# First stage of a four-block kernel: the gate network is multiplied into the mean weights, VectorE normalises three chunks, the orders are rewritten

## The reference

```python
x = x + _layernorm(_L0_attn_ref(_layernorm(x)))          # dilated attention, segments of 64
x = x + _layernorm(_L0_ffn_ref(_layernorm(x), weight))   # Hadamard, 4-bit activations, ternary weights
x = x + _layernorm(_L1_attn_ref(_layernorm(x), ...))     # 16 heads; rows gated, only 32 a batch
x = x + _layernorm(_L1_ffn_ref(_layernorm(x), ...))      # causal attention, 8 experts, top 2

# inside _L1_attn_ref:
q_mean = q.mean(axis=1)                                  # mean over the 16 heads: 64 numbers a token
mu, var = q_mean.mean(-1), q_mean.var(-1)
H = (q_mean - mu) * rsqrt(var + LN_EPS) * ln_g + ln_b
h = gelu(H @ w1.T + b1)                                  # 64 -> 16
scores = (h @ w2.T + b2)[..., 0]                         # one score a token, then the top 32
```

## Time and profile before

| | us |
|---|---|
| median of 3 runs | 642.27 |
| lowest, highest | 640.2, 647.02 |
| the profiled execution | 641.33 |
| its span, first to last instruction | 639.6 |

### The profile page before, as it was taken

One profiled execution on the slowest core, in us unless ns is written; L12 is line 12 of the kernel. 1 busy time (PEld: TensorE's weight loads), 2 busy tenths in 40 slices (PEclk: granted clock), 3 DMA queues, 4 the chain that ended last, 5 costly groups with the idle time before them and its releaser, 6 DMA issues. The chain is left out here.

```text
span 639.6 us, 11630 instructions
## 1 busy us (share of the span) xinstructions
PE 536.4 (84%) x3754; PEld 299.9 (47%) x3754; DVE 485.3 (76%) x2125; ACT 369.1 (58%) x829; POOL 248.8 (39%) x474
## 2 busy tenths in 40 slices
PE   1876577977989997679999999999998898999971
PEld 0876567975676563112333333333333455456420
DVE  6499878367665667889799999999997156369786
ACT  4962255610534564014687788878788665466864
POOL 2001044744001333102445454544555454266764
PEclk9987665557997998555899999999999989899996
DMA  8000000110000694200111111111110000000001
GB/s 325 9 1 2 0 34 35 66 26 8 1 2 9 169 250 130 62 3 5 32 39 37 34 38 35 55 45 39 32 40 2 7 2 1 1 2 17 17 34 66
DMA packets 18875, 27.32 MB, mean 43 GB/s; under 512 B 3230, under 2 KB 14126, under 8 KB 18638
## 3 DMA queue, kind: packets, MB, share of 16 engines
q1 hardware_dynamic: 18174, 24.34, 12.9%
q10 hardware_dynamic: 576, 2.10, 0.9%
q0 software_dynamic: 64, 0.13, 0.1%
HBM read 14.11 MB, written 12.45 MB: 42 GB/s over the span
## 5 line engine op out<-in xcount | busy, mean ns | idle before, releaser
L982 DVE CUSTOM_DVE_ANT_0 w_qkvT<-d_pS,w_qkvT 128x512 bf16<-128x512 f32 x480 | 203.9, 486 | 16.8 <-PE d_pS L973 11.7
L1651 ACT ACTIVATE d_P<-pT 128x768 f32<-128x768 f32 (+1 forms) x192 | 165.9, 882 | 62.7 <-PE pT L1677 61.0
L1531 POOL TENSOR_SCALAR_AFFINE_SELECT d_P<-d_P 128x256 f32<-128x256 f32 x256 | 103.1, 417 | 133.6 <-ACT d_P L1651 133.6
L973 PE MATMUL d_pS<-Ks,Qs 48*128 48x512 bf16 x480 | 97.9, 325 | 12.8 <-DVE hadamard L982 8.9
L1677 PE MATMUL d_pO<-d_P,V 128*32 128x512 f32 (+3 forms) x1024 | 98.5, 460 | 1.4 <-POOL d_P L1531 0.9
L1677 PE MATMUL pT<-Qs,Ks 51*128 51x512 bf16 (+3 forms) x512 | 72.8, 312 | 2.0 <-ACT d_mT L1621 2.0
L973 PEld LDWEIGHTS d_pS<-Ks,Qs 48*128 48x128 bf16 x480 | 32.3, 96 | 56.1 <-DVE hadamard L982 51.9
L1677 PEld LDWEIGHTS pT<-Qs,Ks 51*128 51x128 bf16 x512 | 20.7, 94 | 74.1 <-ACT d_P L1651 42.7
L982 DVE DVE_READ_ACCUMULATOR2_ANT hadamard<- 128x1 f32 x512 | 42.7, 83 | 0.0
L1994 ACT ACTIVATE e_T<-pT,comb 128x128 f32<-128x128 f32 x88 | 25.1, 381 | 22.7 <-issue 15.0
L1677 PEld LDWEIGHTS d_pO<-d_P,V 128*32 128x32 f32 x1024 | 21.2, 110 | 32.3 <-issue 29.5
(11 more groups left out here) (336 smaller groups left out, 1051.7 us busy)
## 6 DMA issues: line engine op xcount, KB each, us to landing
Qs<-q_stack SPq DMA_DIRECT2D x32, 192.0 KB, 3.2
q_stack<-Qp SPq DMA_DIRECT2D x8, 384.0 KB, 2.7
X<-in_x_dram ACTq DMA_DIRECT2D x4, 512.0 KB, 6.2
n_rows<-N SPq DMA_DIRECT2D x4, 512.0 KB, 2.8
q_stack<-Qp SPq DMA_DIRECT2D x8, 256.0 KB, 3.0
out_dram<-e_moe SPq DMA_DIRECT2D x8, 256.0 KB, 2.0
w_qkvT<-in_w_qkvT_dram SPq DMA_DIRECT2D x1, 1536.0 KB
Ks<-k_stack SPq DMA_DIRECT2D x32, 48.0 KB, 3.3
```

The costliest lines, as they stand in the source:

```text
L973: last = nc.tensor.matmul(dst[:, at:at + w], top.Qs[c][rows, h % 8, 128 * q:128 * q + 128], top.Ks[c][rows, h // 4 % 2, 0:w], start=True, ...
L982: last = nc.vector.tensor_tensor_reduce(out=junk[:, at:at + w], in0=src[:, at:at + w], in1=top.wide_mask[:, 512 - w:512], scale=1.0, scala ...
L1531: last = nc.gpsimd.affine_select(out=view, in_=view, compare_op=ALU.is_ge, fill=0.0, base=0, pattern=[[0, 2], [1, 128]], channel_multiplie ...
L1651: nc.scalar.activation(P[pair % 4][:, :, P_AT[unit]:P_AT[unit] + w], pT[(3 * pair + unit) % 2][:, :, 0:w], ACT.Exp, scale=float(HD4) ** -0 ...
```

## The change

The gate network is folded into the mean weights. Its gain and first layer come to a 64 x 16 matrix: the w1 columns times `ln_g`, with the centring over the 64 features applied by `spread`. With the mean weights, turned, on the other side, one product gives `fold`: 64 columns of centred mean queries and 16 columns of first-layer outputs without scale. `means` makes all 80 columns. Since the 64 columns are centred, ACT's `squares3` gives their variance; DVE scales the 16 columns by the reciprocal root and adds a constant row `offset`, made from `ln_b`, w1 and b1. `qstats`, `qnorm`, ACT's `normalise3`, `turned_z`, `gained`, PE's `gate` and POOL's `ones_row` go.

Three of the chunk normalisations are done by DVE, with one tensor_scalar a tile: the first block's of chunks 1 and 3 (from ACT), the third block's of chunk 3 (from POOL). The orders of DVE, ACT and PE are written anew. No transfer is added or taken away; SP's fourth store waits for DVE instead of POOL.

```diff
-        HT = [flat(expS[c])[0:DH + 1, :] for c in chunks]
+        pre = [nT[c][:, 3, :].rearrange("p (t k) -> p t k", k=PROJ) for c in chunks]
...
-        z = [flat(top.O4[:, CT // 2 * c:CT // 2 * c + CT // 2, :]).rearrange("p (t d) -> p t d", d=DH) for c in chunks]
...
+        turned_mean = PS[0][0:DH, 5, :]
+        gain_psum = PS[0][0:DH, 6, 0:PROJ]
+        offset_psum = PS[0][:, 7, 0:PROJ]
+        fold_psum = PS[0][:, 4, 0:DH + PROJ]
+        w_meanT = ph.sb("w_meanT", [DH, D])
+        gains = ph.sb("gains", [DH, PROJ])
+        spread = ph.sb("spread", [DH, DH + PROJ])
+        biases = ph.sb("biases", [DH + 1, D])
+        fold = ph.sb("fold", [128, DH + PROJ])
+        offset = ph.sb("offset", [128, PROJ])
...
-                    sp.wait_ge(sm["s3_n"], done[c])
+                    if c == CHUNKS - 1:
+                        sp.wait_ge(sm["s3_n_vector"], 1)
+                    else:
+                        sp.wait_ge(sm["s3_n"], done[c])
...
+                    nc.vector.tensor_scalar(spread[:, 0:DH], top.ident[0:DH, 0:DH], 1.0 / DH, None, ALU.subtract)
+                    nc.vector.tensor_scalar(gains[:, :], top.w1T[0:DH, :], top.ln_gb[:, 0:1], None, ALU.mult)
+                    dve.wait_ge(sm["ones"], 1 + 1)
+                    nc.vector.tensor_scalar(biases[0:DH, :], biases[0:DH, :], top.ln_gb[:, 1:2], None, ALU.mult)\
+                        .then_inc(sm["fold_rows"], 1)
...
                     dve.wait_ge(sm["parts_psum"], 1)
-                    dve.wait_ge(sm["centred_psum"], 1)
+                    dve.wait_ge(sm["gain_psum"], 1)
+                    nc.vector.tensor_copy(w_meanT[:, :], turned_mean)
+                    nc.vector.tensor_copy(spread[:, DH:DH + PROJ], gain_psum).then_inc(sm["turned"], 1)
+                    nc.vector.tensor_copy(offset[:, :], offset_psum).then_inc(sm["offset_row"], 1)
...
-                    nc.vector.tensor_copy(top.w_qmeanT[:, :], centred).then_inc(sm["centred"], 1)
+
+                def fold_home():
+                    dve.wait_ge(sm["fold_psum"], 1)
+                    nc.vector.tensor_copy(fold[:, :], fold_psum).then_inc(sm["fold"], 1)
...
+                def normalise1(c):
+                    for t in range(CT):
+                        last = nc.vector.tensor_scalar(n[c][:, t, :], X[c][:, t, :], mv["s1_"][c][:, t, 0:1],
+                                                       rs1[c][:, t:t + 1], ALU.subtract, ALU.mult)
+                    last.then_inc(sm["s1_n_vector"], 1)
...
-                def qstats(c):
-                    dve.wait_ge(sm["s3_qm"], done[c])
-                    moments(lambda t: PS[c][:, t, 0:DH], c, "s3_q")
-                    dve.wait_ge(sm["s3_qmv"], done[c])
+                def normalise3(c):
+                    dve.wait_ge(sm["s3_rstd"], done[c])
+                    dve.wait_ge(sm["s1_O"], done[c])
+                    for t in range(CT):
+                        last = nc.vector.tensor_scalar(n[c][:, t, :], X[c][:, t, :], mv["s3_"][c][:, t, 0:1],
+                                                       rs3[c][:, t:t + 1], ALU.subtract, ALU.mult)
+                    last.then_inc(sm["s3_n_vector"], 1)
...
+                def qvariance(c):
+
+                    dve.wait_ge(sm["s3_qss"], done[c])
                     dve.wait_ge(sm["s3_small"], done[c])
-                    nc.vector.tensor_tensor(qvar[c][:, :], mv["s3_q"][c][:, :, 1], small3[c][:, :], ALU.add)\
+                    nc.vector.scalar_tensor_tensor(out=qvar[c][:, :], in0=ss[c][:, :], scalar=1.0 / DH,
+                                                   in1=small3[c][:, :], op0=ALU.mult, op1=ALU.add)\
                         .then_inc(sm["s3_qvar"], 1)
 
-                def qnorm(c):
+                def gate(c):
+
                     dve.wait_ge(sm["s3_qstd"], done[c])
                     nc.vector.reciprocal(qrs[c][:, :], qstd[c][:, :]).then_inc(sm["s3_qrstd"], 1)
                     dve.wait_ge(sm["s3_qrstd"], done[c])
-                    nc.vector.scalar_tensor_tensor(out=qnb[c][:, :], in0=mv["s3_q"][c][:, :, 0], scalar=-1.0,
-                                                   in1=qrs[c][:, :], op0=ALU.mult, op1=ALU.mult)\
-                        .then_inc(sm["s3_qnorm"], 1)
+                    nc.vector.tensor_tensor(pre[c], PS[c][:, :, DH:DH + PROJ],
+                                            qrs[c][:, :].rearrange("p (t o) -> p t o", o=1).broadcast_to([128, CT, PROJ]),
+                                            ALU.mult).then_inc(sm["s3_gate"], 1)
+                    dve.wait_ge(sm["s3_gate"], done[c])
+                    dve.wait_ge(sm["offset_row"], 1)
+                    nc.vector.tensor_tensor(pre[c], pre[c],
+                                            offset[:, :].rearrange("p (o k) -> p o k", o=1).broadcast_to([128, CT, PROJ]),
+                                            ALU.add).then_inc(sm["s3_pre"], 1)
...
-                stats1(0); stats1(1); norm1(0); stats1(2); norm1(1); stats1(3)
-                norm1(2); ternary_weights(); norm1(3); mean_weights(); sums(0); sums(1)
+                stats1(0); stats1(1); norm1(0); stats1(2); norm1(1); normalise1(1); norm1(2)
+                stats1(3); ternary_weights(); norm1(3); normalise1(3); mean_weights(); sums(0); sums(1)
                 ostats1(0); ostats1(1); add1(0); add1(1); stats2(0); stats2(1)
                 sums(2); sums(3); variance1(2); quantise(0); variance1(3); add1(2)
-                weights_home(); add1(3); clamp(0); quantise(1); stats2(2); variance2(0)
-                quantise(2); add2(0); stats2(3); stats3(0); quantise(3); qstats(0)
-                clamp(1); qnorm(0); clamp(2); clamp(3); norm3(0); variance2(1); add2(1)
-                variance2(2); stats3(1); add2(2); norm3(1); variance2(3); stats3(2)
-                add2(3); qstats(1); qnorm(1); stats3(3); norm3(2)
-                qstats(2); norm3(3); qnorm(2); qstats(3); qnorm(3)
+                weights_home(); add1(3); fold_home(); clamp(0); quantise(1); stats2(2); clamp(1)
+                variance2(0); stats2(3); add2(0); quantise(2); variance2(1); add2(1)
+                quantise(3); clamp(2); stats3(0); clamp(3); stats3(1); norm3(0); norm3(1)
+                variance2(2); add2(2); variance2(3); add2(3); qvariance(0); stats3(2); stats3(3)
+                gate(0); qvariance(1); norm3(2); norm3(3); gate(1); normalise3(3)
+                qvariance(2); gate(2); qvariance(3); gate(3)
...
-                def normalise3(c):
-                    act.wait_ge(sm["s3_qnorm"], done[c])
+                def squares3(c):
+                    act.wait_ge(sm["s3_qm"], done[c])
                     for t in range(CT):
-                        last = nc.scalar.activation(z[c][:, t, :], PS[c][:, t, 0:DH], ACT.Identity,
-                                                    bias=qnb[c][:, t:t + 1], scale=qrs[c][:, t:t + 1])
-                    last.then_inc(sm["s3_z"], 1)
...
-                def gained(c):
...
-                    act.wait_ge(sm["s3_zT_psum"], done[c])
-                    nc.scalar.activation(HT[c][0:DH, :], PS[c][0:DH, :, :].rearrange("p t d -> p (t d)"),
-                                         ACT.Identity, bias=top.ln_gb[:, 1:2], scale=top.ln_gb[:, 0:1])\
-                        .then_inc(sm["s3_H"], 1)
+                        last = nc.scalar.activation(nT[c][:, t, 0:DH], PS[c][:, t, 0:DH], ACT.Square,
+                                                    accum_out=ss[c][:, t:t + 1])
+                    last.then_inc(sm["s3_qss"], 1)
...
                     act.wait_ge(sm["s3_pre"], done[c])
-                    nc.scalar.activation(u[c], PS[c][:, 0, :].rearrange("p (t k) -> p t k", k=PROJ), ACT.Gelu)\
+                    nc.scalar.activation(u[c], pre[c], ACT.Gelu)\
                         .then_inc(sm["s3_gelu"], 1)
...
-                std_1(0); std_1(1); normalise1(0); std_1(2); normalise1(1); normalise1(2)
-                copy1(0); std_1(3); copy1(1); normalise1(3); copy1(2); exponential(0)
-                exponential(1); copy1(3); ostd_1(0); ostd_1(1); exponential(2); exponential(3)
+                std_1(0); std_1(1); normalise1(0); std_1(2); copy1(0); normalise1(2); std_1(3); copy1(1)
+                exponential(0); exponential(1); copy1(2); copy1(3); ostd_1(0); ostd_1(1)
+                exponential(2); exponential(3)
                 copy2(0); squares1(2); std_2(0); std_2(1); squares1(3); copy2(1)
                 ostd_1(2); ostd_1(3)
-                copy2(2); copy2(3); std_2(2); squares2(0); ostd_2(0); copy3(0); std_2(3)
-                std_3(0); qstd_3(0); normalise3(0); squares2(1); ostd_2(1); squares2(2); gained(0)
-                ostd_2(2); copy3(1); std_3(1); squares2(3); ostd_2(3); copy3(2); qstd_3(1)
-                normalise3(1); std_3(2); copy3(3); std_3(3); gained(1); qstd_3(2)
-                normalise3(2); qstd_3(3); normalise3(3); gained(2); gelu(0); gelu(1); gained(3)
-                gelu(2); gelu(3)
```

(58 more changed lines are left out.)

12 lines of the change are left out of this document (5 added, 7 removed), and 6 rows, old and new, of the table sm.

## The result

The median of four runs is 620.22 us (619.95 to 624.36); the kernel before has 642.26 us. The ratio is 0.9664, 95% interval 0.9619 to 0.9708. The profiled execution took 620.27 us, 21.06 less than the one before. The predicted time, 626 us, is 5.8 us too high; it is inside its range of 619.5 to 634, near the lower end, and next to rival A (621 us).

The account below looks back on a forecast made before the run. DVE's order while busy, then a slackless chain at the end, bound the first stage. Start 5.33 + work 95.8 + gaps 3.4 + waits 10.0 gave 114.5 us, 16.1 less: 626 us, range 619.5 to 634.

Parts of the forecast that it names:

- rival A: Last normalisation of the first stage: POOL does not hold DVE's tensor_scalars, 5.25 us go, 621 us; chance 0.12.
- two signs that the prediction named for itself: First stage's end and after: `normalise3(3)` at 7 us or more while POOL runs; the stage after unchanged.
- Sign and mechanism of the gain: First stage: DVE's work rises from 93.57 to 95.8 us, less waiting makes the stage 16.1 us shorter.
- Front: Start of the first stage: normalising and weights fill DVE's 3.3 + 4.9 us of waits; 0.9 us is left.
- Middle: Second block of the first stage: DVE's 6.9 us wait for squares goes; costed at no wait.
- the thin covers: Second block, first stage: DVE's work ahead of `variance2(2)` and `variance2(3)` covers the squares by 0.75 and 0.4 us.
- Rival B: Second block of the first stage: `variance2` waits as before, 6.9 us return, 633 us; chance of 630 to 635: 0.15.
- Before the last gates: Late first stage: `norm3(2)` on DVE waits 1.5 us for ACT's `copy3(3)` and `std_3(2)`, queued behind `qstd_3(1)`.
- The collision: Late first stage: POOL's row of eight tensor_scalars holds DVE's `normalise3(3)` until it ends, 5.25 us.
- Tail: End of the first stage: waits of 0.25 us (variance, root), 0.95 (squares), 0.3 (root) and 0.8 (GELU) left.
- The following stages are as before: Stages behind the first: unchanged, so the first stage's 16.1 us carry to the total.
- Rival E: Later stages, 350 to 450 us: PE's clock falls; 16 us at that level cancels the gain; chance 0.04.

Follow-up runs that it names:

- fold-only: The kernel before with the gate network folded into the mean weights, old orders, no chunk moved to DVE: median 633.01 us, ratio 0.9854.
- front-only: The kernel before with DVE normalising the first block's chunks 1 and 3, and new orders up to the second attention products: 638.03 us, ratio 0.9928.
- the table: The changed kernel plus fourteen steps behind the first stage's last score, DVE's eight instructions beside different POOL work or none: 681.84 us with the added work.
- after: The changed kernel, with the whole change, against the kernel before it: median 620.22 us, ratio 0.9664.
- before: The kernel without the change, against which ratios are taken: 642.26 us.

## Why the prediction was right, and where not

*Sign and mechanism of the gain: right.* DVE's work was to be 95.8 us (94.85), and the gain to come from waits: 10.0 us of them were to be left besides the input, 5.2 were. The fold-only and front-only runs show two of its parts apart. But the time itself was missed by 5.8 of 22 us, and two signs that the prediction named for itself failed: `normalise3(3)` took 2.29 us and not 7, and the stage behind changed its length.

*Front:* one wait of 0.9 us was forecast behind the root of the fourth chunk; it is 0.8, at line 216. A normalised chunk on DVE: 2.2 us against 2.13.

*Middle:* no wait of DVE for the second block's squares; the thin covers of 0.75 and 0.4 us held. Rival B is out. The three waits for `ostd`, 0.8 us together, I had not named; they were costed at nothing.

*Before the last gates:* 1.5 us forecast, 1.4 measured, and the kernel that takes its cause away gives back 1.34.

*The collision: the term that failed.* 5.25 us taken, 0.16 measured; that is 5.1 of the 5.5 us between the forecast end of the stage, 114.5 us, and the real one, 108.98. (The rest is small: DVE's work 1.1 us less than summed, the other waits 0.5 us more, the start 0.2 us later.) The step was "a row of instructions without gaps is what held `selT`". What held `selT` was that POOL ran memsets. The row of 247.36 is of another kind as well, a POOL tensor_tensor; neither row said anything of a POOL tensor_scalar. A sum without the collision was in the range, as rival A; I gave it 0.12. That the range holds the measured time is owed to this bound and not to the forecast. The one DVE instruction in the rows beside this very operation, the add of 0.19 us in the earlier trace rows, had shown no hold, though it was a tiny one. The Trainium skill (SBUF — State Buffer, section SBUF: two separate sides) has DVE and GpSimd exclude each other for a whole instruction when DVE uses both ports. By that, with a turn after each of POOL's instructions, the chunk would have taken about 6.4 us; the measurement, 2.29, decides against it for this operation. For POOL's adds the table agrees with it: eight small ones take 3.33 us and DVE's eight beside them 3.34, one for one. Memsets hold DVE too, but its turn can come only after several of them.

*Tail:* forecast 0.25 + 0.95 + 0.3 + 0.8; the rows have 0.8 for the last variance, 0.6 for two roots and 0.8 for the GELU, 2.2 against 2.3. The last two products of 80 columns, 16 matmuls each, take 3.70 and 3.71 us, the 64-column one of the earlier trace rows 3.52: not quite nothing, but hidden.

*"The following stages are as before": wrong by 2.0 us.* Rival E had the mechanism, the clock in later stages, but looked at another stretch and priced it at 16 us and more; it came as a small loss in the second stage beside a gain of 21.6. With the collision at its 0.16 us the sum would have been 620.9 us. That this is so close to the measured 620.2 is partly luck: the 2.0 us lost to the clock were made up by 1.1 us in later stages, by small terms of the first, and by 0.9 us that I had added because the median before lay above the profiled execution, which it did not do after.

Open stays what decides when the clock rises in the second stage. With PE's work there the same, and the wait of 2 to 3 us ahead of the product, the 10 us from 20 us on came out at 1.00, 0.83 or 0.66. The traces show the course, not the cause: in eight profiled executions, `after` among them, the clock had risen ahead of the wait and fell again near its end; in `before` it rose with the wait already begun and stayed; with the fold alone it rose only at 148.25 us, in the middle of the product. With the wait at 0.5 us, or filled, it did not fall. The idle time of PE ahead of the stage does not decide it: it is 3.0 us both in the kernel before (1.00) and with the front alone (0.66). The starting time does not either. Whether it would differ between executions of one kernel I can't say, since each was profiled once; for the first stage, where one code drew 1.00 and 0.85, it does, and why is open too.
